# Rounds written out, and the order of work inside a step of the attention pass, in a decoder layer's kernel

## What is computed

```python
x = x + attn(layernorm(x))    # three softmaxes: causal, means of 4 keys, the top 64 of 256 kept
x = x + xattn(layernorm(x))   # cross attention over the 512 columns of a 256-channel context,
                              # 8 heads of 32, relative position terms within 4 of the diagonal
x = x + ffn(layernorm(x))     # dense 512 -> 1024 -> 512, GELU, and for each of 8 heads one
                              # expert of 8192, found by a product-key search, its rows gathered
```

## Time and profile before

| | us |
|---|---|
| median of 3 runs | 2764.03 |
| lowest, highest | 2760.65, 2766.27 |
| the profiled execution | 2767.55 |
| its span, first to last instruction | 2765.9 |
| TensorE's mean granted clock | 0.971 |

### The profile page before, as it was taken

The page is one execution under the profiler, slowest core; times in us unless marked ns, Lnnn a source line. Parts: engine busy times, 40 slices in busy tenths (PEclk is TensorE's granted clock), DMA queues, the critical chain, the costliest instruction groups (busy, mean ns, idle before and its releaser), DMA issues. The chain is left out here.

```text
span 2765.9 us, 47489 instructions
## 1 busy us (share of the span) xinstructions
PE 2422.7 (88%) x12792; PEld 1328.5 (48%) x12792; DVE 2073.4 (75%) x5959; ACT 1093.5 (40%) x2559; POOL 1009.2 (36%) x1486
## 2 busy tenths in 40 slices
PE   7889988988889898899885999998989898989975
PEld 4455555655556555555553644443434343434432
DVE  1467676666766667667642299998989998989997
ACT  2266666656666666666663211111111111111110
POOL 1133333233332333333221245554445444445542
PEclk9999999999999999999997999999999999999997
DMA  3044454434544345443544899998989999998996
GB/s 103 16 119 116 121 161 132 138 106 123 160 133 139 106 123 157 136 139 106 154 128 144 302 363 383 380 377 327 377 326 377 354 381 349 359 377 339 378 369 248
DMA packets 303986, 631.20 MB, mean 228 GB/s; under 512 B 162800, under 2 KB 167920, under 8 KB 303728
## 3 DMA queue, kind: packets, MB, share of 16 engines
q0 software_dynamic: 79616, 423.66, 40.1%
q1 hardware_dynamic: 190320, 103.92, 13.2%
q10 hardware_dynamic: 33792, 100.67, 11.0%
HBM read 581.99 MB, written 146.80 MB: 263 GB/s over the span
## 5 line engine op out<-in xcount | busy, mean ns | idle before, releaser
L1078 DVE CUSTOM_DVE_ANT_0 scores<-s_bank,added 128x512 f32<-128x512 f32 x512 | 350.3, 688 | 273.2 <-PE s_bank L581 190.6
L1417 PE MATMUL l_bank<-fold,xn_tf 128*128 128x512 f32 x1024 | 449.9, 592 | 2.8 <-ACT xn_tf L1492 2.8
L886 ACT ACTIVATE probs<-scores,nmx 128x512 f32<-128x512 f32 x512 | 372.8, 728 | 151.5 <-DVE nmx L1078 148.3
L1377 POOL DMA_INDIRECT out_rows<-rows_out,rows_now x256 | 259.4, 1013 | 375.5 <-DVE res L1658 303.1
L892 ACT COPY prob_t<-t_bank 128x512 f32<-128x512 f32 x512 | 298.4, 583 | 210.5 <-PE t_bank L591 210.5
L519 POOL TENSOR_TENSOR added<-mask_add,band 128x136 f32<-128x136 f32 (+1 forms) x512 | 245.4, 481 | 362.2 <-DVE nmx L1078 360.8
L1367 POOL DMA_INDIRECT in_rows<-rows_in,rows_now x256 | 292.7, 1143 | 223.1 <-DVE hid L1628 133.3
L591 PE MATMUL t_bank<-ident,probs 128*128 128x128 f32 x2048 | 315.0, 281 | 8.4 <-ACT cv L864 4.1
L1505 ACT COPY sims<-l_bank 128x512 f32<-128x512 f32 x128 | 74.2, 580 | 626.1 <-PE l_bank L1417 626.1
L591 PEld LDWEIGHTS t_bank<-ident,probs 128*128 128x128 f32 x2048 | 234.5, 142 | 180.0 <-issue 104.1
L1417 PEld LDWEIGHTS l_bank<-fold,xn_tf 128*128 128x128 f32 x1024 | 194.3, 190 | 247.3 <-issue 243.8
(11 more groups left out here) (179 smaller groups left out, 3630.9 us busy)
## 6 DMA issues: line engine op xcount, KB each, us to landing
rows_in<-in_in_b_dram ACTq DMA_DIRECT2D x16, 2048.0 KB, 8.9
rows_out<-in_out_a_dram ACTq DMA_DIRECT2D x16, 2048.0 KB, 9.0
rows_in<-in_in_a_dram ACTq DMA_DIRECT2D x16, 1024.0 KB, 5.8
rows_out<-in_out_b_dram ACTq DMA_DIRECT2D x16, 1024.0 KB, 5.4
x_scratch<-x SPq DMA_DIRECT2D x32, 512.0 KB, 7.1
rel_scratch<-rel_pad SPq DMA_DIRECT2D x16, 640.0 KB, 3.2
band<-rel_scratch SPq DMA_DIRECT2D x512, 20.0 KB, 2.1
prob_scratch<-probs SPq DMA_DIRECT2D x512, 20.0 KB, 2.3
```

The costliest lines, as they stand in the source:

```text
L886: nc.scalar.activation(prob_tile(s % PSLOTS), scores[:, s % 2, :], ACT.Exp, bias=nmx[:, s:s + 1], scale=-1.0, accum_out=lsum[:, s:s + 1]). ...
L1078: nc.vector.tensor_tensor_reduce(out=scores[:, s % 2, :], in0=s_bank[s % HPT][:, 0:L], in1=added[:, s % 2, :], scale=-1.0, scalar=-NEG, op ...
L1377: nc.gpsimd.indirect_dma_start(out_rows[:, h, :], None, rows_out, bass.IndirectOffsetOnAxis(rows_now[:, odd, h:h + 1], 0)).then_inc(out_lo ...
L1417: ins = nc.tensor.matmul(l_bank[c % 2][:], xn_t[:, k, :], fold[:, k, c * BANK:(c + 1) * BANK], start=(k == 0), stop=(k == KD - 1))
```

## The change

Three things are changed.

1. The loops are gone: every round of both passes is written out, semaphore targets are constants, and the `gate` increments are removed.
2. In the attention pass's steps, TensorE's `turn` comes ahead of `score`, and `spread` is last; ScalarE's copies for `finish`, `attend_second` and `attend_first` come ahead of `exponentials`, the exponentials of the self attention come last of all (`self_exponentials`), and `keep_spread` moves from lag 6 to lag 7.
3. The K products (`CK`) move from `attend_first` (steps 30 and 31, a sequence ahead) to the end of `attend_second` (steps 28 and 30, the same sequence as CV). `c_in` is loaded at step 31 instead of 26, behind the semaphore `c_used` that ScalarE raises after the second K copy.

```diff
@@ class At
-        V, TOP, CK, LOAD_C = (17, 27), 20, (30, 31), 26
+        V, TOP = (17, 27), 20
-        CV, REL, LOAD_MASK, MASK = (22, 25), 23, 4, 26
+        CV, REL, LOAD_MASK, MASK, CK, LOAD_C = (22, 25), 23, 4, 26, (28, 30), 31
-    TURN_LAG, SUM_LAG, SPREAD_LAG, WEIGH_LAG, EVICT_LAG = 3, 5, 6, 8, 9
+    TURN_LAG, SUM_LAG, SPREAD_LAG, KEEP_LAG, WEIGH_LAG, EVICT_LAG = 3, 5, 6, 7, 8, 9
@@ attention_pass (and the same in expert_pass)
-        def rounds(round_, eng):
-            for b in (-1, 0, 1):
-                round_(b, b % 2)
-            with eng.Fori(1, B // 2 - 1) as i:
-                round_(2 * i, 0)
-                round_(2 * i + 1, 1)
-            for b in range(B - 2, B + 2):
+        def rounds(round_):
+            for b in range(-1, B + 2):
                 round_(b, b % 2)
@@ GpSimd
             def load_c(b):
-                pool.wait_ge(cv_done, b)
-                nc.gpsimd.sem_inc(gate, 1)
+                pool.wait_ge(c_used, b)
@@ TensorE
                 if s == 0:
-                    pe.wait_ge(t_emptied, t_job(r, "CQ", CT - 1)[1] + 1)
+                    pe.wait_ge(t_emptied, t_job(r, "CK", CT - 1)[1] + 1)
...
                 for s in range(STEPS):
+                    if turn_at(b, s):
+                        turn(b, s, *turn_at(b, s))
                     if s % HPT == 0 and cross_in_round(b):
                         score(b - 1, s, p)
-                    if turn_at(b, s):
-                        turn(b, s, *turn_at(b, s))
                     if tail_in_round(b):
                         finish(b, s)
-                    if group_at(b, s, SPREAD_LAG):
-                        spread(*group_at(b, s, SPREAD_LAG))
                     if group_at(b, s, WEIGH_LAG):
                         weigh(b, s, *group_at(b, s, WEIGH_LAG), cv[:, 1 - p if s >= WEIGH_LAG else p])
...
                     if first_in_round(b):
                         attend_first(b, s, p)
+                    if group_at(b, s, SPREAD_LAG):
+                        spread(*group_at(b, s, SPREAD_LAG))
@@ ScalarE
                     if turn_at(b, s):
                         turned(b, s, *turn_at(b, s))
-                    if group_at(b, s, SPREAD_LAG):
-                        keep_spread(*group_at(b, s, SPREAD_LAG))
-                    if cross_in_round(b):
-                        exponentials(b - 1, s)
+                    if group_at(b, s, KEEP_LAG):
+                        keep_spread(*group_at(b, s, KEEP_LAG))
...
                     if second_in_round(b):
                         attend_second(b, s, p)
                     if first_in_round(b):
                         attend_first(b, s, p)
+                    if cross_in_round(b):
+                        exponentials(b - 1, s)
+                    self_exponentials(b, s)
@@ ScalarE, attend_second (the K copy, from attend_first)
+                if s in At.CK:
+                    o = At.CK.index(s)
+                    bank = t_full(b, "CK", o)
+                    nc.scalar.activation(ck[:, p, o, :], bank[:, 0:L], ACT.Identity,
+                                         bias=cb_k[:, o:o + 1]).then_inc(t_emptied, 1)
+                    if o == CT - 1:
+                        act.sem_inc(c_used, 1)
@@ VectorE, top_score (one of many such places)
                 wait(dve, exp_done, r * STEPS + s - 1)
-                dve.sem_inc(gate, 1)
```

More of the change, by code:

```diff
@@ L435, in round_ @@
                     near_back(r)
-            rounds(round_, sp)
+            rounds(round_)
             sp.wait_ge(x2_stored, B * 16)
@@ L552, in _ @@
             nc.gpsimd.memset(probs[:], 0.0).then_inc(probs_zeroed, 1)
-            rounds(round_, pool)
+            rounds(round_)
         @block.tensor
@@ L688, in attend_second @@
                     ins.then_inc(t_filled, 1)
+                if s in At.CK:
+                    o = At.CK.index(s)
+                    bank = t_open(b, "CK", o)
+                    product(bank[:, 0:L], lambda k: cw_k[:, k, o * P:(o + 1) * P], lambda k: c_in[:, k, :],
+                            CT).then_inc(t_filled, 1)
             def finish(b, s):
@@ L838, in attend_first, with self_exponentials @@
                     nc.scalar.copy(v[:, t, :], bank[:, 0:D]).then_inc(a_emptied, 1)
-                if s in At.CK:
-                    o = At.CK.index(s)
-                    bank = t_full(b, "CK", o)
-                    nc.scalar.activation(ck[:, 1 - p, o, :], bank[:, 0:L], ACT.Identity,
-                                         bias=cb_k[:, o:o + 1]).then_inc(t_emptied, 1)
-            def attend_second(b, s, p):
-                if s == At.E_S:
-                    for t in range(TT):
-                        act.wait_ge(sparse_ready, b * TT + t + 1)
-                        nc.scalar.activation(e_s[:, t, :], left[:, t, :], ACT.Exp, bias=nmax[:, t, 2:3],
-                                             accum_out=sums[:, t, 2:3]).then_inc(exps_ready, 1)
+            def self_exponentials(b, s):
+                c = b + 1
+                if first_in_round(b):
+                    if s in (At.E_W, At.E_W + 2):
+                        t = (s - At.E_W) // 2
+                        act.wait_ge(nmax_ready, c * TT + t + 1)
+                        nc.scalar.activation(e_w[:, t, :], causal[:, t, :], ACT.Exp, bias=nmax[:, t, 0:1],
+                                             accum_out=sums[:, t, 0:1])
+                        nc.scalar.activation(e_c[:, t, :], csum[:, t, :], ACT.Exp, bias=nmax[:, t, 1:2],
+                                             scale=1.0 / COMP, accum_out=sums[:, t, 1:2])
+                if second_in_round(b):
+                    if s == At.E_S:
+                        for t in range(TT):
+                            act.wait_ge(sparse_ready, b * TT + t + 1)
+                            nc.scalar.activation(e_s[:, t, :], left[:, t, :], ACT.Exp, bias=nmax[:, t, 2:3],
+                                                 accum_out=sums[:, t, 2:3]).then_inc(exps_ready, 1)
+            def attend_second(b, s, p):
                 if s == At.WT:
@@ L966, in _ @@
             act.wait_ge(f_emptied, f_job("U") + 1)
-            rounds(round_, act)
+            rounds(round_)
         @block.vector
@@ L1159, in _ @@
             dve.wait_ge(f_emptied, f_job("U") + 1)
-            rounds(round_, dve)
+            rounds(round_)
 def expert_pass(nc, w, x2_dram, x3_dram, out, rows_in, rows_out, rows_laid):
@@ L1267, in expert_pass @@
         res_stored = sem("res_stored")
-        gate = sem("gate_f")
         def nothing_after(r, ahead):
@@ L1276, in nothing_after, with rounds @@
             return isinstance(r, int) and r + ahead >= ROUNDS
-        def rounds(step, eng):
-            for r in range(RING):
-                step(r, r)
-            with eng.Fori(1, ROUNDS // RING - 1) as i:
-                for j in range(RING):
-                    step(RING * i + j, j)
-            for r in range(ROUNDS - RING, ROUNDS):
+        def rounds(step):
+            for r in range(ROUNDS):
                 step(r, r % RING)
@@ L1342, in _ @@
                 load_tokens(r, r)
-            rounds(step, sp)
+            rounds(step)
             sp.wait_ge(res_stored, 16 * ROUNDS)
@@ L1381, in _ @@
             pool.wait_ge(rows_laid, 4 * 16 * w["x"].shape[0])
-            gathers(0, 0)
-            gathers(1, 1)
-            with pool.Fori(1, ROUNDS // 2 - 1) as pair:
-                gathers(2 * pair, 0)
-                gathers(2 * pair + 1, 1)
-            gathers(ROUNDS - 2, 0)
-            gathers(ROUNDS - 1, 1)
+            for r in range(ROUNDS):
+                gathers(r, r % 2)
         @block.tensor
@@ L1479, in _ @@
             turn_tokens(2, 2)
-            rounds(step, pe)
+            rounds(step)
         @block.scalar
@@ L1545, in _ @@
             take_tokens(2)
-            rounds(step, act)
+            rounds(step)
         @block.vector
@@ L1717, in _ @@
             self_wait(dve)
-            rounds(step, dve)
+            rounds(step)
 def decoder_layer(nc, w, out):
```

53 lines of the change are left out of this document (9 added, 44 removed).

## The result

| kernel | median us | lowest to highest | runs | ratio to before, 95% interval |
|---|---|---|---|---|
| before | 2765.15 | 2760.65 to 2770.39 | 4 | |
| changed | 2679.05 | 2675.82 to 2680.30 | 4 | 0.9686 [0.9666, 0.9706] |

The change makes the kernel 86.1 us (3.1%) faster; 2684 had been forecast. The total is right, but by luck and not as a sum of the right terms: the experiments show that the loops and the gates gave all of it, and the new order of the steps nothing.

A forecast was written before the change was run, and what follows sets the result against it. TensorE was taken to bound full attention rounds and VectorE the expert pass. Loops 37.8 + 10.3, attention rounds 25 (1.8 each over fourteen), ends 4.7 + 2 made 80 us: 2764 - 80 = 2684, range 2630 to 2722.

The forecast's parts named there:

- loops: Both passes: writing rounds out removes back-edge holes, 37.8 us in the expert pass and 10.3 in the attention pass, 48.1 together.
- gates (with register arithmetic): Dropping gate increments and register arithmetic: nothing in the expert pass, 0.3 us in each attention round.
- Rival D: Straight code also waits for instructions: 2745 to 2806 us; chances 0.04 without overall loss, 0.02 slower.
- Spread last and the K products: Attention round's end: 2.21 us of TensorE holes can go, GpSimd's delay may lose 0.5; 0.9 us a round taken.
- no wait for `ck`: A sign the forecast is right: TensorE no longer waits for ScalarE's copies of the K products in the attention pass.
- Copies ahead of exponentials: Attention rounds: earlier copies save 0.3 us a round at step 5's output product and 0.3 at all other eviction waits.
- ScalarE's waiting: Attention steps: ScalarE waits for TensorE's product before that step's exponentials; charged 0, bounds 0 and 2 us a round.
- Turns ahead of scores: Attention pass: a turn fits in the scores' wait but stays on the path; 0 taken, bounds 0 and 1.65 us a round.
- Ends: Attention pass: rounds -1 and 0 gain 4.7 us; rounds 15 and 16 gain 4 less 2, net 2.
- B: Rival: the order gives far more, attention holes shrink by 5 us a round; 2639 us, near 2600 at most; chance 0.11.
- C: Rival: slower, ScalarE becomes the path as copies hold up exponentials, 6 us a round lost; 2807 us; chance 0.06.
- A: Rival: the order gives nothing, filled holes reappear at VectorE or GpSimd; 2711 us, up to 2722; chance 0.16.

The follow-up runs named there:

- e1: The kernel before with only its loops written out in both passes; 2705.87 us, ratio 0.9787 to the kernel before.
- e2: e1 with the gate increments removed too, order of work and K products as before; 2676.31 us, ratio 0.9681 to the kernel before.
- u5: The changed kernel with GpSimd's load of `c_in` put behind `add_bo` and the first `added`; 2684.64 us, ratio 0.9704 to the kernel before.
- u4: The changed kernel with ScalarE's exponentials, self attention's too, ahead of its copies again at all steps; 2677.63 us, ratio 0.9671 to the kernel before.
- v1: The changed kernel with ScalarE's exponentials ahead of the V copy at step 17 alone; 2655.69 us, ratio 0.9606 to the kernel before.
- u1: The changed kernel with TensorE's scores ahead of the turn again; 2695.57 us, ratio 0.9730 to the kernel before.
- u3: The changed kernel with K products back at steps 30 and 31, a sequence ahead, load at 26; 2667.73 us, ratio 0.9635 to the kernel before.
- u2: The changed kernel with TensorE's spread ahead of the step's products again; 2685.20 us, ratio 0.9704 to the kernel before.
- e3: The kernel before, loops and gates kept, with the new step order and the K products' move; 2775.83 us, ratio 1.0036 to the kernel before.
- w1: The changed kernel with K products back as in u3 and exponentials first at all steps as in u4; 2696.44 us, ratio 0.9760 to before.
- x1: The changed kernel with u3 and v1 together; 2641.32 us, ratio 0.9542 to the kernel before.
- w2: e2 with the K products' move, `keep_spread` at lag 7 and self attention's exponentials with the others; 2684.48 us, ratio 0.9718 to before.

## Why the prediction was right, and where it was not

| part | forecast us | measured us | by |
|---|---|---|---|
| loops | 48.1 | 60.9 | before to e1 |
| gates (with register arithmetic) | 4.2 | 29.6 | e1 to e2 |
| order, K products, ends | 27.7 | -2.7 | e2 to the changed kernel, of another group (-1.4 by the ratios; the intervals overlap) |
| sum | 80 | 87.8 (86.1 by the medians of its own group) | |

- **Loops.** The back edges were worth what their rows said: 38.1 us in the expert pass for 37.8. Rival D is refuted: in e1 and in the changed kernel VectorE, which sets the pace of the expert pass, has no "issue" wait of more than 0.2 us in it. (TensorE has 46.6 us of "issue" there in e1, and none is listed in the changed kernel; a round takes 35.3 us with 34.87 of VectorE busy, so it cost nothing.) By the rule of the Trainium skill cited there (DMA: Bandwidth & Descriptors, "Queues, rings and completion order") a refill, which has the runtime's own queue row, takes its turn with the gathers' packets; no run here shows that this costs anything in straight code, at a DMA share of 0.99. The share put under "register arithmetic" was too small: 1.0 us a straight attention round came with the loops. What in the loop's body makes it (addresses worked out in registers, waits on register values) was not taken apart.
- **Gates.** The step that failed most is "in the expert pass they are dispatched while VectorE computes, so they cost nothing now". They cost 0.5 us a round, a little over the 0.44 named as the bound, since VectorE's busy time falls too (34.87 to 34.66). In the attention pass they cost 0.9 where 0.3 was charged for gates and registers together. The view had shown a part of it: of the 0.44 us of idle in a round that waits for nothing, 0.3 went with the gates.
- **Spread last and the K products, 0.9 a round.** The spread gives 0.4. The K products' part has the wrong sign: up to -0.8. The 2.21 us of holes did go; in their place stand two waits for `ck` and longer ones for `prob_t`, `nmx` and `cq`. The delay charged to GpSimd, 0.5, is not the loss; u5 leaves it 0.2 at most. Nor did the mark "no wait for `ck`" come: there are 24 of them, 6.9 us.
- **Copies ahead of exponentials, 0.3 and 0.3.** `g_t`'s wait fell from 1.0 to 0.6 us a round, about the 0.45 worked out for it. The other evictions gained far more than the 0.3 counted, beside the other edits. Against u4, the same kernel with exponentials first, TensorE's two waits for `xn_t` fall from 26.3 to 9.9 us in twelve rounds, `ck` from 9.1 to 6.9, `cv` from 4.1 to nothing that is listed: with `g_t` 2.4 us a round (`cq` stays at 9.3). The next term takes it all back.
- **ScalarE's waiting, 0.** This is the mis-sized term: step 17 was named as one of the tightest places, with bounds of 0 and 2 us a round, and 0 was taken. The V copy at step 17 alone makes it 1.5 (v1); against u4, the waits for `prob_t` and for scores together are 2.5 us a round longer. The row for it stood in the profile of before: a product of eight matmuls takes 3.6 to 3.7 us, longer than the 2.7 us of a step.
- **Turns ahead of scores, 0.** Also wrong: with score first (u1) the waits of scores are 34.8 us, with turn first 6.1. With step 17 put right as well, the round falls from 84.2 to 81.7; what each order of turn and score gives there is not shown, since no run has score first with step 17 put right. "Every turn still lies once on the path" doesn't hold, since the turn ran in time in which TensorE waited.
- **Ends.** Round 1 starts 4.8 us earlier than in u3 (139.9, not 144.7), close to the forecast 4.7. How much of this is the K products is less sure: with them moved round 1 starts between 139.3 and 143.2 (146.5 in v1), otherwise between 144.7 and 146.4. Round 15 loses 5.3, not 2: it is not bound by TensorE, but a product there isn't hidden either.

So the profile showed the marks of B (score waits that vanish) and of C (turns that wait for ScalarE) at once, and they cancelled. A, the order giving nothing, was the true account of the order, at a chance of 0.16; it was hidden in the total because the gates were undercharged by 25 us and the loops by 13, which the 30 us too many for the order nearly cancelled. That is luck: with the order's true worth of nothing and these two charges the forecast would have been A's 2711.

## What to carry to other kernels

Where one engine empties banks and also makes the next operands, one fixed order of the two need not suit every step, as here: at each step, ask which of them is ready first, and let that one go first. A product of 3.7 us before the copy says exponential first; scores that come late say copy first. Edits of order aren't worth the sum of their parts, so after each one look for the new largest wait, and time combinations. Bare semaphore increments and loop bookkeeping look free beside busy engines, but part of the idle time that no wait explains can be theirs; here it was 0.3 of 0.44 us in an expert round.

## What the runs showed of the hardware

A long hole of TensorE can be paid for twice: by itself, and by a dip of the granted clock right behind it. Windows of the changed kernel, behind the 1.70 us hole in a round where the clock fell, and over the hole in one where it held:

```profile
610.50:613.50 3.00, 3.00 (x19) 1.48 (x12) 2.59 (x12) 0.10 (x1) 0.51 (x2) 0.79 1.06 323
```

```profile
521.50:531.50 10.00, 7.96 (x67) 4.33 (x64) 6.90 (x26) 7.72 (x24) 3.38 (x8) 1.00 0.84 274
```

Such a dip lengthens a round by 1.6 us, with the same work. It came in 4 of 12 rounds behind the 1.70 us hole, in 4 to 6 of 12 in u2, u3 and u5, which have the same hole, in only 1 of 12 in e3, whose hole is as long, and in 11 of 12 rounds behind w1's hole of 2.16 us. There the K product right behind the hole took 3.35 us, mostly at a granted clock of 0.50, and the one ahead of it 1.96 at 1.00: the lower of the two levels, 1.2 and 2.4 GHz, against the upper one. In the kernel before it came behind two of the five back edges, holes of 2.1 us. In v1 and x1, with that hole gone, none of the rounds 2 to 13 has one, and none had in e1, e2 and u1. In u4 (5 rounds) and w2 (3), without the 1.70 us hole, dips came at the start of some rounds, behind several shorter holes close together (0.9 and 1.3 us in u4, 0.7, 0.7 and 0.3 in w2). Why it comes in one round and not in the next with the same holes stays open.
